# Loading the weight units of five projections in pairs and fours instead of one by one

## What is computed

```python
def attn(x, ...):                 # x: layer-normed input
    xn = x * rsqrt(mean(x * x) + EPS) * norm_w
    u = (xn @ in_w.T + in_b) * sigmoid(xn @ gate_w.T + gate_b)   # 1024 -> 2048
    b = u @ b_w.T + b_b           # 2048 -> 2048
    c = u @ c_w.T + c_b           # 2048 -> 2048
    d = u @ d_w.T + d_b           # 2048 -> 2048
    h_t = a * h_(t-1) + b_t       # scan over the 4096 tokens
    y = (c * h + d) @ out_w.T + out_b                            # 2048 -> 1024
    return x + y
def ffn(x, ...):                  # 1024 -> 3072 -> 1024
    return (silu(x @ wg.T) * (x @ wu.T)) @ wd.T
x = x + attn(layernorm(x)); x = x + ffn(layernorm(x))
```

## Time and profile before

| what | value |
|---|---|
| three runs | 3817.26, 3935.75 and 3525.8 us; median 3817.26 |
| the profiled execution | 3415.96 us |
| its span, slowest core (7) | 3414.4 us; the eight cores 3393.8 to 3414.4 |
| mean granted TensorE clock | 0.987 to 0.990 |
| PE busy | 3156.3 us of the span |
| bytes moved by the DMA queues | 545.82 MB, 160 GB/s on average |

### The profile page before, as it was taken

One profiled execution on the slowest core, in us unless ns is written; L12 is line 12 of the kernel. 1 busy time (PEld: TensorE's weight loads), 2 busy tenths in 40 slices (PEclk: granted clock), 3 DMA queues, 4 the chain that ended last, 5 costly groups with the idle time before them and its releaser, 6 DMA issues.

```text
span 3414.4 us, 39744 instructions; the slowest of 8 cores (3393.8 to 3414.4 us)
## 1 busy us (share of the span) xinstructions
PE 3156.3 (92%) x14328; PEld 1401.9 (41%) x14328; DVE 1036.9 (30%) x1466; ACT 526.8 (15%) x778; POOL 202.8 (6%) x388
## 2 busy tenths in 40 slices
PE   1887777899999999999999999999999999999999
PEld 0333333344444444344444444444444444444444
DVE  3221214132242223422333323422234223332231
ACT  0110111111211111111211112111111112111120
POOL 0011000000100001000010001000010000100010
PEclk9999998999999999999999999999999999999999
DMA  5899998653446434454345544464345543454344
GB/s 111 194 215 217 216 215 219 185 163 114 148 145 207 154 110 152 171 177 152 113 141 187 168 124 139 151 203 151 105 159 179 178 150 112 147 173 161 117 142 130
DMA packets 153840, 545.82 MB, mean 160 GB/s; under 512 B 17456, under 2 KB 17456, under 8 KB 153648
## 3 DMA queue, kind: packets, MB, share of 16 engines
q1 hardware_dynamic: 98352, 325.16, 28.1%
q0 software_dynamic: 55296, 218.13, 25.3%
HBM read 526.44 MB, written 73.40 MB: 176 GB/s over the span
## 4 chain that ended last, share of the span: by engine, by line
PE 73%; DMA 16%; DVE 7%; issue 2%; ACT 1%; DVEq 0%; SPq 0%; POOLq 0%; ACTq 0%; POOL 0%
PE pb L279 73%; DMA s_wa<-dw_wd 3%; DMA s_wa<-dw_wfu 2%; DMA s_wa<-cw_wug_in 2%; DMA cw_wd<-s_wa 2%; DMA cw_wfu<-s_wa 2%; DVE s_xn L360 1%; DMA s_x<-x 1%; DVE s_sr L358 1%; DVE s_sr L356 1%; DVE s_w L369 1%; DMA s_wa<-dw_wug_g 1%; DMA s_wa<-dw_wout 1%; DMA cw_wfd<-s_wa 1%; DMA s_wa<-dw_wfd 1%
## 5 line engine op out<-in xcount | busy, mean ns | idle before, releaser
L279 PE MATMUL pb<-s_uy,s_wa 128*128 128x512 bf16 x8704 | 1921.2, 382 | 107.8 <-DVE s_x L636 25.8
L279 PEld LDWEIGHTS pb<-s_uy,s_wa 128*128 128x128 bf16 x8704 | 851.5, 98 | 1167.6 <-issue 170.5
L279 PE MATMUL pb<-s_xn,s_wa 128*128 128x512 bf16 x5120 | 1130.5, 383 | 95.4 <-DVE s_xn L360 28.2
L279 PEld LDWEIGHTS pb<-s_xn,s_wa 128*128 128x128 bf16 x5120 | 501.7, 98 | 722.0 <-issue 136.0
L457 DVE TENSOR_TENSOR_SCAN s_hs<-s_a,s_h,s_bsb 128x512 f32<-128x512 f32 x128 | 164.3, 1284 | 439.4 <-ACT s_bsb L453 438.2
L598 DVE SCALAR_TENSOR_TENSOR s_uy<-pb,s_gsb 128x512 bf16<-128x512 f32 x192 | 132.7, 691 | 535.5 <-PE pb L279 509.5
L429 DVE SCALAR_TENSOR_TENSOR s_uy<-pb,s_bias,s_gsb 128x512 bf16<-128x512 f32 x128 | 96.1, 751 | 391.4 <-ACT s_gsb L425 391.4
L453 ACT ACTIVATE s_bsb<-pb,s_bias 128x512 f32<-128x512 f32 x128 | 88.0, 687 | 800.4 <-PE pb L279 800.4
L595 ACT ACTIVATE s_gsb<-pb 128x512 f32<-128x512 f32 x192 | 114.6, 597 | 547.8 <-PE pb L279 547.7
L486 DVE SCALAR_TENSOR_TENSOR s_uy<-pb,s_bias,s_yv 128x512 bf16<-128x512 f32 x128 | 96.1, 751 | 265.2 <-PE pb L279 265.2
L483 DVE TENSOR_TENSOR s_yv<-s_csb,s_hs 128x512 f32<-128x512 f32 x128 | 88.6, 692 | 246.2 <-ACT s_csb L467 245.0
(11 more groups left out here) (47 smaller groups left out, 639.4 us busy)
## 6 DMA issues: line engine op xcount, KB each, us to landing
s_wa<-cw_wb SPq DMA_DIRECT2D x112, 512.0 KB, 3.6
s_wa<-cw_wc SPq DMA_DIRECT2D x112, 512.0 KB, 3.5
s_wa<-cw_wd SPq DMA_DIRECT2D x112, 512.0 KB, 3.6
s_wa<-cw_wfg POOLq DMA_DIRECT2D x84, 512.0 KB, 3.8
s_wa<-cw_wfu POOLq DMA_DIRECT2D x84, 512.0 KB, 4.8
s_wa<-cw_wfd POOLq DMA_DIRECT2D x56, 768.0 KB, 5.2
s_wa<-cw_wug_in SPq DMA_DIRECT2D x56, 512.0 KB, 4.2
s_wa<-cw_wug_g SPq DMA_DIRECT2D x56, 512.0 KB, 4.6
```

Of the source, the lines that this page charges most:

```text
L279: lambda t: t.matmul(pbank[bi][:], lh, rh, start=st, stop=sp))(),
```

## The change

A load can now cover n units that stand one behind the other in the arena and in the DRAM array. load_w takes n, its slot is n units long from the first unit's place, and the DRAM side is viewed as partition, unit, column. The write-back of such a load is one transfer of n units too. wb, wc and wd are loaded in pairs: units 0 and 1 at the chunk's start as before, units j + 1 and j + 2 after odd rounds j, into both slots at once. wout units 0 to 3 are one load in round 14, units 4 and 5 one after block 1 of the output step, units 6 and 7 one after block 3. The other families, the matmuls and all arithmetic stay. The same is done at the start of chunk 0 and at a chunk's end, and flush_wb writes n units back; these hunks are left out below.

```diff
@@ -210,8 +210,25 @@
         def overlaps(a, b):
             return a[0] < b[0] + b[1] and b[0] < a[0] + a[1]
 
-        def load_w(role, seq, unit, ch, sem=None):
-            slot = slot_of(role, seq)
+        def wb_src(slot, n):
+            sf = slot_flat(slot)
+            if n == 1:
+                return sf
+            return sf.rearrange("p (u j) -> p u j", u=n)
+
+        def cw_view(role, unit, n):
+            if n == 1:
+                return cw[role][unit]
+            return cw[role][unit:unit + n].rearrange("u p j -> p u j")
+
+        def dw_view(role, unit, n):
+            if n == 1:
+                return dw[role][unit]
+            return dw[role][unit:unit + n].rearrange("u p j -> p u j")
+
+        def load_w(role, seq, unit, ch, sem=None, n=1):
+            off = SLOTS[role][seq % len(SLOTS[role])]
+            slot = (off, n * UNIT_SZ[role])
             ws = []
             for oslot in list(occ):
                 if not overlaps(oslot, slot):
...
@@ -220,23 +237,27 @@
                 for r2 in list(o):
                     key2 = (r2, oslot)
                     if key2 in pending_wb:
-                        wunit, ltok = pending_wb.pop(key2)
-                        wtok = em.dma("Q", (lambda r2=r2, wunit=wunit, sf=slot_flat(oslot):
-                                            lambda g: g.dma_start(cw[r2][wunit], sf))(),
+                        wunit, wn, ltok = pending_wb.pop(key2)
+                        wtok = em.dma("Q", (lambda r2=r2, wunit=wunit, wn=wn,
+                                            oslot=oslot: lambda g: g.dma_start(
+                                                cw_view(r2, wunit, wn),
+                                                wb_src(oslot, wn)))(),
                                       waits=[ltok])
                         o.setdefault(r2, []).append(wtok)
                 for lst in o.values():
                     ws.extend(lst)
                 del occ[oslot]
             occ[slot] = {role: []}
+            dst = wb_src(slot, n)
             if ch == 0:
-                tok = em.dma("G", (lambda dst=slot_flat(slot), role=role, unit=unit:
-                                   lambda g: g.dma_start(dst, dw[role][unit]))(),
+                tok = em.dma("G", (lambda dst=dst, role=role, unit=unit, n=n:
+                                   lambda g: g.dma_start(dst, dw_view(role, unit, n)))(),
                              waits=ws, sem=sem)
-                pending_wb[(role, slot)] = (unit, tok)
+                pending_wb[(role, slot)] = (unit, n, tok)
             else:
-                tok = em.dma(FAM_Q[role], (lambda dst=slot_flat(slot), role=role,
-                                           unit=unit: lambda g: g.dma_start(dst, cw[role][unit]))(),
+                tok = em.dma(FAM_Q[role], (lambda dst=dst, role=role, unit=unit,
+                                           n=n: lambda g: g.dma_start(
+                                               dst, cw_view(role, unit, n)))(),
                              waits=ws, sem=sem)
             return tok
 
...
@@ -386,10 +408,9 @@
             fb_ops(st_cur, f)
             fb_w(st_cur, f)
         st_cur["wb"], st_cur["wc"], st_cur["wd"] = {}, {}, {}
-        for j in range(2):
-            st_cur["wb"][j] = load_w("wb", j, j, 0)
-            st_cur["wc"][j] = load_w("wc", j, j, 0)
-            st_cur["wd"][j] = load_w("wd", j, j, 0)
+        for role, d in (("wb", st_cur["wb"]), ("wc", st_cur["wc"]),
+                        ("wd", st_cur["wd"])):
+            d[0] = d[1] = load_w(role, 0, 0, 0, n=2)
 
         wug_in = s_wa[:, 0:4096].rearrange("p (b k j) -> p b k j", b=2, k=DK)
         wug_g = s_wa[:, 4096:8192].rearrange("p (b k j) -> p b k j", b=2, k=DK)
...
@@ -472,14 +493,14 @@
                     mm(bd_, wview("wd", j, IK)[:, k, :], u_v[:, k, :], k == 0, k == IK - 1,
                        waits=[tok_wd[j]] if k == 0 else [], inc=(k == IK - 1))
                 slot_used("wd", j, banks[bd_].w)
-                if j + 2 < IK:
-                    j2 = j + 2
-                    tok_wb[j2] = load_w("wb", j2, j2, c)
-                    tok_wc[j2] = load_w("wc", j2, j2, c)
-                    tok_wd[j2] = load_w("wd", j2, j2, c)
+                if j % 2 == 1 and j + 1 < IK - 1:
+                    j2 = j + 1
+                    for role, d in (("wb", tok_wb), ("wc", tok_wc), ("wd", tok_wd)):
+                        d[j2] = d[j2 + 1] = load_w(role, j2, j2, c, n=2)
                 elif j == IK - 2:
+                    t4 = load_w("wout", 0, 0, c, n=4)
                     for sq_ in range(4):
-                        tok_wout[sq_] = load_w("wout", sq_, sq_, c)
+                        tok_wout[sq_] = t4
                 tok_yv[j] = em.emit("V", (lambda j=j: lambda v: v.tensor_mul(
                     s_yv[:, j % 2], s_csb[:, j % 2], s_hs[:, j % 2]))(),
                     waits=[tok_csb], inc="V")
...
@@ -507,8 +528,9 @@
                     mm(bo, wview("wout", j, IK)[:, k, :], y_v[:, k, :],
                        k == 0, k == IK - 1, waits=ws, inc=(k == IK - 1))
                 slot_used("wout", j, banks[bo].w)
-                if j + 4 < DK:
-                    tok_wout[j + 4] = load_w("wout", j + 4, j + 4, c)
+                if j in (1, 3):
+                    tok_wout[j + 3] = tok_wout[j + 4] = load_w(
+                        "wout", j + 3, j + 3, c, n=2)
                 tok_x1[j] = em.emit("V", (lambda j=j, bo=bo: lambda v: v.scalar_tensor_tensor(
                     s_x1[:, j], pbank[bo][:], s_ob[:, j:j + 1], s_w[:, j],
                     ALU.add, ALU.add))(),
```

More of the change, by code:

```diff
@@ L247, in flush_wb @@
                     continue
-                wunit, ltok = pending_wb.pop(key2)
-                wtok = em.dma("Q", (lambda r2=r2, wunit=wunit, sf=slot_flat(slot):
-                                    lambda g: g.dma_start(cw[r2][wunit], sf))(),
+                wunit, wn, ltok = pending_wb.pop(key2)
+                wtok = em.dma("Q", (lambda r2=r2, wunit=wunit, wn=wn, slot=slot:
+                                    lambda g: g.dma_start(cw_view(r2, wunit, wn),
+                                                          wb_src(slot, wn)))(),
                               waits=[ltok])
@@ L654, in build_nc @@
                 st_next["wb"], st_next["wc"], st_next["wd"] = {}, {}, {}
-                for j in range(2):
-                    st_next["wb"][j] = load_w("wb", j, j, c + 1)
-                    st_next["wc"][j] = load_w("wc", j, j, c + 1)
-                    st_next["wd"][j] = load_w("wd", j, j, c + 1)
+                for role, d in (("wb", st_next["wb"]), ("wc", st_next["wc"]),
+                                ("wd", st_next["wd"])):
+                    d[0] = d[1] = load_w(role, 0, 0, c + 1, n=2)
                 st_cur = st_next
```

## The result

| | before | changed |
|---|---|---|
| profiled execution | 3415.96 us | 3457.9 us |
| its span, slowest core | 3414.4 us (core 7) | 3456.3 us (core 1) |
| range of its eight cores | 3393.8 to 3414.4 | 3435.7 to 3456.3 |
| timed runs | 10, lowest 3418.93 | 9, lowest 3457.2, median 3466.14 |

The changed kernel takes 1.0128 times as long as the one before (95% interval 1.0083 to 1.0174). Runs disturbed by a lowered clock on one die are left out of this ratio; the plain median of before, 3507 us in its ten runs, holds some and is no measure of the change. So the kernel got slower by 1.3%: within the 2% that counts here as the same, but clear of its own interval.

What follows compares the result with a forecast made beforehand. Prediction: DMA throughput bounds chunk 0's B/C/D step, while PE stays busy in chunks 1 to 7 and waits for none of these loads. 3416 + 65.8 - 11 + 2 = 3473 us (+1.7%), range 3440 to 3510.

Steps and rivals of the forecast that it cites:

- The B/C/D step: Chunk 0: seven rounds of 37.1 us each, step 280.5 us against 214.7 before, +65.8 us.
- all of it beside write-backs: Chunk 0's B/C/D rounds: wd's pair loads beside write-backs throughout, taking 9.7 us and landing at 28.0 us.
- The lone load: Chunk 0's B/C/D rounds: wb's pair, loaded alone at first, lands after 9.6 us, so PE waits 2.7 us.
- The clock: Chunk 0's B/C/D rounds: PE runs slower after wd's wait, costing 2.1 us a round, bounds 0 to 2.8.
- The output step: Chunk 0: wout waits fall to 3.2 us from 14.0 plus a 2.2 us slow block, -11 us.
- Chunks 1 to 7: Paired loads land within their lead of 6.9 or 7.8 us; +2 us in all, bounds 0 and 15.
- Steady loads getting late: Rival, chunks 1 to 7: 1 MB loads need 8 us, 54 us lost, 3527 in all; chance 0.17.
- Chunk 0 dearer than worked out: Rival, chunk 0: slower loads and clock add 16 us, 3489 in all; chance 0.15.
- Bigger transfers win: Rival, chunk 0: larger transfers speed the mix from 4.85 to 4.6 us, 3394 in all; chance 0.06.
- No change: Rival: pairs are cut into the old pieces and the third family refills chunk 0's longer rounds, 3416 us; chance 0.04.

Runs made afterwards that it cites:

- e1: Changed kernel with chunk 0 loading as before, pairs and the four-unit load only from chunk 1 on; ratio to before 0.9998.
- e5: Changed kernel with two pair slots for each of wb, wc and wd, so pairs go out earlier; ratio to before 1.0017.
- e11: Changed kernel with 16 dummy matmuls ahead of each pair's first block in chunk 0; B/C/D step 260.2 us against 263.9.
- e2: Changed kernel with wout loaded unit by unit as before; output step of chunk 0 32.4 us against 35.9.
- e3: Kernel before with only wout loaded as a four and two pairs; chunk 0's B/C/D and output steps together 10 us longer than before.
- e4: Changed kernel with each pair split into two one-unit loads at the same issue times; chunk 0's B/C/D step 244.5 us.
- e6: Changed kernel without write-backs of wb, wc and wd in chunk 0, stand-in reads later; chunk 0's B/C/D step 223.3 us.
- e7: Kernel before without write-backs of wb, wc and wd in chunk 0, stand-in reads later; chunk 0's B/C/D step 165.8 us on six cores.
- e8: Kernel before with wc and wfu written back in chunk 1, wd in chunk 2, wfd spread over chunks 0 to 2; ratio 0.9902.
- e9: Kernel before with wc written back in chunk 1, wd and wfu in chunk 2; ratio 0.9878.
- e10: Kernel before with only wc (chunk 1) and wd (chunk 2) written back later; ratio 0.9881.

## Why the prediction was right or wrong

- **The time and the place.** 3473 us were predicted and 3458 measured in the profiled execution, 3466 in the median of its nine runs; within the 3440 to 3510, slower, and by less than 2%. Worked out was +57 us, measured +42, so the loss came out a third too large. The mechanism is the one predicted: e1 puts all of it in chunk 0, e5 gives five sixths of it back by giving back the lead. One reading of before was wrong: in the steady part of the step its loads do not go out at the end of PE's block but some 7 to 8 us later, when the old unit's write-back has landed. The sum did not suffer, since it takes before's step as measured and in the changed kernel PE is what a load waits for.
- **The B/C/D step, +65.8 predicted, +55.9 measured.** This is the term that failed. Seven rounds were to take 37.1 us each (set against 29.2 before, where the rows give 29.1 to 29.6) and took (270.6 - 13.9 - 6.9) / 7 = 35.7: the first six 34.7, the last 41. Two parts of the round were too dear. The first is that wd's data run "all of it beside write-backs" at 4.85 us a unit, to land 28.0 us after wb's issue. In the first six rounds they landed after 24.7 to 27.1 us, 26.0 on average, although wb's pair, at 10.7 us, was later than the 9.6 worked out. Between these two landings the queues moved this (first round, 184.7 to 201.1 us; the queue of the loads, then that of the write-backs: packets, MB, share of 16 engines):

```profile
q0 software_dynamic: 511, 1.96, 76.5%
q1 hardware_dynamic: 433, 1.71, 26.9%
```

  That is 3.7 units loaded and 3.3 written in 16.4 us: 4.4 us for a unit loaded, not 4.85, and at 224 GB/s for both, not 216. Loads and write-backs do not share evenly, as I had taken from before (24.7 units of each in 120 us), where both queues always held two or three. That the number waiting in each queue sets the parts fits this; it was not tried. The second part is the clock, below. The last round was longer than worked out: its wd pair landed 31.5 us after wb's issue, with the four-unit wout load queued behind it. In sum: wd's landing 12 us less over six rounds, the clock 6.6 less, the last landing 3.5 more, and 5 more for the 0.75 us a round between landing, PE's blocks and the next issue, for which the sum had no term; together the 10 us.
- **The lone load.** Fixed part and 3.2 us a unit gave a wait for wb of 2.7 us. On the slowest core a second unit added 4.3 us to the landing (10.7 against 6.4), and the waits were 4.9 us; on core 0 they were 1.6 to 2.1 in four rounds of seven and 3.0 to 4.4 in the others. The term lay between the two kinds of core, and the slowest one counts.
- **The clock, 2.1 us a round behind wd's wait.** The seven stretches behind it took 8.1 us more than at full speed in sum (13.97 is full speed for 64 matmuls, the worst took 16.89), 1.2 a round. Behind three of the waits, of 1.7 to 2.6 us, nothing was lost; behind the other four, of 3.1 to 4.7 us, 1.3 to 2.9 each. That is 8.1 us where the sum had 14.7. That the other two waits hide theirs is right, by e11.
- **The output step, -11 predicted, -13.4 measured.** Right in size. But the prediction let it read as what the four-unit load does; e2 and e3 show that the emptied queues do it, and e3 that this load costs 10 us where the queues are full.
- **Chunks 1 to 7, +2 predicted, -2.2 measured** on different cores, +0.4 on average. 1 MB landed after 4.8 us, where 5.0 to 5.6 were worked out (a further unit at 393 GB/s is 1.3 us, not 1.4), and after 5.7 at POOL, for 6.2. The Trainium skill ("DMA: Bandwidth & Descriptors", Anatomy of one DMA) states its fit for DMAs issued from GpSimd; the 4.4 us by it are 1.3 below what POOL's loads took, and 0.4 below SP's.
- **The rivals.** Steady loads getting late: falls by the landing and by e1. Chunk 0 dearer than worked out: the reverse. Bigger transfers win: falls twice; with the lead kept (e5) the engines move 218 GB/s, no more than before, and the time is 1.0017. The Trainium skill's "Double-buffer for performance" ("Trainium Kernel Development and Optimization", Best Practices) is what the changed kernel gives up and what e5 puts back; its rule of 1 MiB per DMA ("DMA: Bandwidth & Descriptors", Rules for kernel authors) brought no rate here (218 against 216 GB/s). That several loads of 512 KB were in the queue at once anyhow would explain it; this was not tried alone. No change: falls.

## What to carry to other kernels

Merging two refills of a two-slot buffer into one halves nothing but the number of DMAs and takes away the second buffer: before merging, compare the lead that is left (here 6.9 us) with the landing time in the busiest chunk (10.7 us), not in the usual one (4.8). Ask also what a load waits for, since it can change with the merge: here from a write-back, which ran beside PE's blocks, to the blocks themselves. Where the DMA engines are the bound, look for what need not be moved there: shifting two families' write-backs into chunks whose B/C/D step has DMA share 0.42 to 0.43 took 1.2% off, where changing the size of the transfers gave nothing. A gain that shows beside a loss (the output step) is to be tested alone before it is credited.

## What was unexpected of the hardware

- The cores fall into two kinds. In the changed kernel cores 1, 2, 5 and 6 take 269.8 to 270.9 us for the B/C/D step and cores 0, 3, 4 and 7 take 255.8 to 259.0: one of each neighbouring pair. Core 0 waits 1.6 to 2.1 us for dw_wb in each of the first four rounds, where core 1 waits 4.3 to 5.7. Before, with full queues, all eight lay within 211.0 to 214.7. The slowest core is the metric, so it pays the dearer kind. Which core of a pair it is changes with the execution: in e4 cores 1, 2, 4 and 7, in e11 cores 0, 3, 4 and 7. In all four pairs of the changed kernel and of e2, e4, e6 and e11 it is the one that reached the step later, by 0.6 to 5 us, each counted from its own first instruction. That the two cores of a pair share something on their way to memory would fit; no run took one of them away, and it stays open.
- With PE never waiting, two cores of e7 ran the step at a lowered clock and six did not. Cores 4 and 5 needed 193 us, the others 165.8, so e7's average of 172.6 in the table holds 7 us of this. The windows of core 5 (the first row) beside core 3:

```profile
200.00:250.00 50.00, 50.00 (x192) 20.66 (x190) 11.53 (x16) 5.50 (x8) 6.33 (x12) 0.81 0.76 126
```

```profile
160.00:360.00 200.00, 198.90 (x923) 89.93 (x921) 59.69 (x88) 31.07 (x47) 29.79 (x56) 1.00 0.95 157
```

  A granted clock of 0.81 for over 100 us with PE busy all the time is not the fall behind a wait; cores 0 and 1 had the same in e8 (core 1: 0.81 from 160 to 260 us), a neighbouring pair again, and no core stands out so in e9 and e10. It weighs up to 27 us on one execution, and its cause is open.
